# Local attention in blocks of 32 queries by 64 keys: scores on eight TensorE tiles, values on four, one PSUM bank for all fills

## The chip, the cores and the metric

One core of one Trainium2 chip. The metric is the device time of one execution in microseconds (us), the median of three runs. The core has TensorE (PE, matrix products), VectorE (DVE), ScalarE (ACT), GpSimd (POOL) and SyncE (SP, which issues DMA transfers). TensorE writes into PSUM, which has eight banks of 128 partitions by 512 fp32 numbers; the others read PSUM and on-chip memory. Each engine works off its own program in order and waits on semaphores for the others. An fp32 product shows as two records in the trace.

## What is computed

The kernel is a chain of eight stages on x of 8 sequences x 256 tokens x 128 features, each as `x = x + layernorm(stage(layernorm(x)))`: a memory-augmented attention, a linear split, a linear attention, a mixture of experts, a Mamba layer, a grouped-query attention block, a latent attention ("mla") and, last, the local transformer that the change is about. Of that last one, for each of six layers:

```python
DIM, DEPTH, HEADS, DIM_HEAD, WINDOW = 128, 6, 16, 64, 32
DIM_INNER, QK_SCALE = int(DIM * 4 * 2 / 3), 8.0        # 341
...
def look(t):                       # each window of 32 keys and the one before it
    p = jnp.pad(t, ((0, 0), (0, 0), (1, 0), (0, 0), (0, 0)))
    return jnp.concatenate([p[:, :, :nw], p[:, :, 1:]], axis=3)
bk2, bv2 = (look(bk), look(bv))
mask = (it < jb) | (it > jb + w) | (jb == -1)
sim = jnp.einsum('bhwie,bhwje->bhwij', bq, bk2) * QK_SCALE
sim = jnp.where(mask, -jnp.finfo(sim.dtype).max, sim)
attn = jax.nn.softmax(sim, -1)
out = jnp.einsum('bhwij,bhwje->bhwie', attn, bv2)
...
q = l2norm(q) * qs                 # then rotary embedding; k likewise
...
xn = (x - mu) / jnp.sqrt(var + 1e-05) * g + bln
a, gate = jnp.split(xn @ W1 + b1, 2, -1)
return a * jax.nn.gelu(gate, approximate=False) @ W2 + b2
```

## The kernel before

**Units and steps.** The local stage (`stage_local`) runs 48 units, one for each layer and sequence. A unit `n` has eight steps `p = 0..7`, one for each pair of heads; step `s = 8n + p`. Parts of several units are under way at once: in step `s` the program makes raw q or k rows for the part `s + 16` (two units ahead), turns the rows of part `s + 5`, makes the scores of `s`, turns the probabilities of `s - 2` and makes the values of `s - 3`.

**TensorE's program in a step, in this order.** The mask (L3115, one bf16 product of 384 columns that puts the bias into the score bank), eight score products (L3118: blocks of 64 queries by 96 keys for two heads, on 64x64 tiles of the array, two at a time), early fills, four flips of probabilities (L403, `table,xn`) and four of rows (L403, `table,scratch`), half the output projection at p = 2 and 3 (L3145), the centering at p = 5 (L3150), eight value products (L3162: 128 keys by 64 features, on 128x64 tiles), late fills, and last the raw rows (L3176, 512 columns). Fills are the products of the layer's other work: V (L3068, p = 4 to 7), moment (L3073), ones (L3078), gates (L3083), third (L3088, L3089), linear (L3092) and out (L398, three products). Gates, linear and third are the parts of the gated MLP of width 341 = 128 + 128 + 85, and third holds both halves of the last 85.

**Banks.** Raw rows have bank 0; the scores of step s bank 2 + s % 2; turned probabilities bank 4; turned rows bank 5; values and centering share bank 6. Fills have two banks: 7 for project, third, ones and moment, 1 for the rest. `Bench.plan` puts down for each fill which semaphore tells that its bank has been read, and `wait_free` waits for that of the fill before in the same bank.

**VectorE in a step.** Exponent sum of s - 1 with its reciprocal (L3326, L3328), rope on the raw rows (L3277, L3279, L3280), maximum of the scores (L3340), squared lengths (L3360) and small work of the MLP and residuals (L3352, L3370, L3377, L3384, L3385). At p = 5 and 7 it runs the inverse root of a row of lengths (`dve_root`, L3299 to L3311, twelve operations, each waiting for the one before), after the lengths.

**ScalarE in a step.** Square of the raw rows (L3226, the last reader of the raw bank: TensorE's next raw product waits on `squared`), copy of the turned probabilities (L3231), four exponentials (L3236), copy of the turned rows (L3248), copy of the sums (L3253), copies of V (L3191), and at p = 0 three gelus of a unit (L3209), for which the activation table is loaded, and loaded back for the next exponentials. **GpSimd** adds the rope's halves (L3432), divides the probabilities (L3425) and scales rows by the inverse root (L3439). **SyncE** moves parts of V to other partitions, three transfers in a unit.

Of the kernel before, what the change touches and what calls it, by code (L numbers as in the profile page):

```python
# [7 lines left out]
P = 128  # L8
F32 = mybir.dt.float32
U32 = mybir.dt.uint32  # L10
BF16 = mybir.dt.bfloat16
# [12 lines left out]
EPS = 1e-5  # L24
# [93 lines left out]
def layout(i):  # L118
# [42 lines left out]
    for l in range(DEPTH):  # L161
# [6 lines left out]
        out[f"layer{l}"] = [("wqkv", a[m + "Wqkv"][l]), ("wo", chunks(a[m + "Wo"][l])), ("w1", w1),  # L168
# [7 lines left out]
def tables():  # L176
# [9 lines left out]
    def near(b):  # L186
        i, j = np.arange(P)[:, None] % 64, np.arange(96)[None, :] - 32
        return np.where((j <= i) & (j >= i - LWIN) & (64 * b + j >= 0), 0, NEG).astype(f)
# [4 lines left out]
            ("band", np.concatenate([near(b) for b in range(4)], axis=1))]  # L193
# [264 lines left out]
def dve_see(M, first, n, signal, k):  # L458
# [6 lines left out]
    M.seen = first + n  # L465

# [127 lines left out]
def stage_titan(M):  # L594
# [388 lines left out]
    def pool_program():  # L983
        M.wait_loaded(pool, "titan")
        nc.gpsimd.tensor_copy(xT[:, TOKENS:], w("memT")).then_inc(S("mem_copied").up(), 1)
# [379 lines left out]
def act_rows(A, s):  # L1365
# [4 lines left out]
    for g in range(4):  # L1370
        if 0 <= u < A.units:
            n = 4 * u + g
            act.wait_ge(S("bounded"), n // 2)
# [13 lines left out]
def dve_rows(A, s):  # L1387
    M, nc, dve, S = A.M, A.M.nc, A.M.dve, A.M.sig
    for n in range(4 * s, 4 * s + 4):
        if s < A.units:  # L1390
# [5 lines left out]
            for t in range(2):  # L1396
                half = x[:, SEQ * t:SEQ * t + SEQ]
                nc.vector.tensor_tensor_reduce(half, half, A.factor[:, SEQ * t:SEQ * t + SEQ], A.scale, -3.0e38, ALU.mult, ALU.max,
                                               A.low[s % 3][:, 2 * g + t:2 * g + t + 1]).then_inc(dve.link(), 1)
            if g % 2:  # L1400
                pair = A.low[s % 3][:, 2 * g - 2:2 * g + 2]
                dve.settle()
                nc.vector.tensor_scalar(pair, pair, -1.0, None, ALU.mult).then_inc(S("bounded").up(), 1)
# [1561 lines left out]
BLOCKS, QB, KB = 4, 64, 96  # L2965
PAIRS_L = LHEADS // 2
WIDTH = BLOCKS * KB


def stage_local(M):  # L2970
# [18 lines left out]
    rows, V = M.ring(2, 8, 512), M.ring(2, BLOCKS, LIN)  # L2989
    KT, QT = M.ring(2, PAIRS_L, KB - QB + SEQ), M.ring(2, PAIRS_L, SEQ)  # L2990
    sines, sq = M.alloc(512), M.ring(2, 512)
    E, probs, turned, sums = M.ring(2, BLOCKS, KB), M.ring(2, BLOCKS, P), M.ring(2, BLOCKS, P), M.ring(PAIRS_L, SEQ)
    small, lengths = M.ring(4, 2, BLOCKS), M.ring(2, 3, 66)
    rope = M.ring(2, 4, 2, LDIM)
    xc, sq2, fed, dg, gl = M.alloc(SEQ), M.alloc(SEQ), M.alloc(SEQ), M.alloc(2, P), M.alloc(3, SEQ)
    ident, mask = M.alloc(P // 2).bitcast(BF16), M.alloc(WIDTH // 2).bitcast(BF16)
# [7 lines left out]
    score_bank = lambda s: M.bank(2 + s % 2)[:, 0:WIDTH]  # L3004
    blocks = lambda ap: ap.rearrange("p (b k) -> p b k", b=BLOCKS)
    over_keys = lambda ap: ap.unsqueeze(2).broadcast_to([P, BLOCKS, KB])
    TURNED, PARTS_T = M.bank(4), M.bank(5)

    SUMS, CENTER = M.bank(6)[:, 0:SEQ], M.bank(6)[:, SEQ:]
# [10 lines left out]


    rooms = [Bench(M, (1,)), Bench(M, (7,))]

    def bench_of(key):
        return rooms[key in ("project", "third", "ones", "moment")]

# [500 lines left out]
```

## Time and profile before

| | |
|---|---|
| median of 3 runs | 4085.57 us (4078.26 to 4090.87) |
| profiled execution | 4084.84 us, span 4083.5 us, mean granted clock of TensorE 0.937 |
| busy over the span | PE 3410.5 us (84%), DVE 2945.7 (72%), ACT 2254.4 (55%), POOL 1544.3 (38%) |
| seven stages ahead of the local one | 0 to about 1976 us |
| local stage | about 1976 to 4060 us, of it 2100 to 4000 in steady state |

A row of the timeline gives start and duration in us, the engine, the line of the kernel, the operation with the names and shapes of its output and inputs, how many records follow each other (x4), and in brackets how long the engine had been idle and what ended that. A shape such as `64*64` behind the names is the tile of the TensorE array. Busy times of TensorE overlap by the depth of its pipeline, so prices are read from start to start.

### The profile page before, as it was taken

Reading aid. Unit: us, or ns where it says so; the run is one execution under the profiler, and the core shown is the slowest. Engines: PE = TensorE matmul, PEld = TensorE weight load, DVE = VectorE, ACT = ScalarE, POOL = GpSimd, SP = SyncE. Lnnn points to the kernel's source line nnn. Section 1 sums busy time; section 2 is a strip of 40 time slices with the busy share of each in tenths; the row PEclk is TensorE's granted clock in tenths of the full one; section 3 lists DMA queues with packets and bytes.
Section 4 is the critical chain, followed back from the end, with each engine's and each line's share of the span. In section 5 each row is a group of like instructions: output and inputs, shape, how many; then the busy total and the mean of one; then the engine's idle time right before and its main releaser. Section 6 shows DMA issues by size and latency. Waiting matters only on the chain.

```text
span 4083.5 us, 78115 instructions
## 1 busy us (share of the span) xinstructions
PE 3410.5 (84%) x29021; PEld 2239.7 (55%) x29021; DVE 2945.7 (72%) x7904; ACT 2254.4 (55%) x5408; POOL 1544.3 (38%) x1445
## 2 busy tenths in 40 slices
PE   6878856457767798775799999999999999999997
PEld 4544535323234465443466666666666666666665
DVE  6465675457875455796888887887888888888875
ACT  4234433256543322686466666666666666666664
POOL 0110012436640000001655555555555555555551
PEclk9989977778889989898899999999999999999998
DMA  1000004510000000000000010001001000100000
GB/s 52 1 5 1 1 25 121 147 40 0 0 5 1 1 1 28 1 2 28 14 21 14 16 39 23 18 17 42 18 17 41 20 15 15 48 15 18 17 14 18
DMA packets 34218, 94.04 MB, mean 23 GB/s; under 512 B 5057, under 2 KB 15169, under 8 KB 32049
## 3 DMA queue, kind: packets, MB, share of 16 engines
q1 hardware_dynamic: 31312, 83.87, 7.1%
q0 software_dynamic: 2528, 5.18, 0.7%
q8 instruction: 232, 3.80, 0.4%
q14 instruction: 146, 1.19, 0.1%
HBM read 52.40 MB, written 5.18 MB: 14 GB/s over the span
## 4 chain that ended last, share of the span: by engine, by line
PE 37%; DVE 30%; ACT 15%; issue 6%; POOL 2%; DMA 1%; POOLq 0%; SPq 0%; ACTq 0%; DVEq 0%
PE psum L398 6%; PE psum L403 5%; PE psum L3145 4%; PE psum L1133 4%; PE psum L3176 3%; DVE scratch L3277 3%; ACT y L3236 3%; PE psum L1985 3%; PE psum L3162 2%; PE psum L3118 2%; DVE scratch L3326 2%; DVE scratch L3279 2%; ACT L3209 1%; ACT L3236 1%; PE psum L1187 1%
## 5 line engine op out<-in xcount | busy, mean ns | idle before, releaser
L3432 POOL TENSOR_TENSOR scratch<-scratch 128x512 f32<-128x512 f32 x384 | 489.0, 1273 | 261.0 <-DVE scratch L3280 261.0
L3425 POOL TENSOR_TENSOR xn<-y,scratch 128x384 f32<-128x384 f32 x384 | 317.6, 827 | 638.4 <-DVE scratch L3328 638.2
L3226 ACT ACTIVATE y<-psum 128x512 f32<-128x512 f32 x384 | 229.4, 597 | 592.7 <-DVE scratch L3280 592.7
L3176 PE MATMUL psum<-weights,scratch 128*128 128x512 f32 x768 | 413.7, 621 | 33.4 <-ACT y L3226 20.4
L403 PE MATMUL psum<-table,scratch 128*128 128x128 f32 (+1 forms) x2260 | 367.1, 283 | 80.3 <-ACT scratch L3248 32.0
L403 PE MATMUL psum<-table,xn 128*128 128x128 f32 x1648 | 270.7, 292 | 188.1 <-DVE xn L485 186.6
L3236 ACT ACTIVATE y<-psum,scratch 128x96 f32<-128x96 f32 x1536 | 401.8, 354 | 14.0 <-DVE scratch L3340 13.3
L3326 DVE TENSOR_REDUCE scratch<-y 128x4 f32<-128x384 f32 x384 | 211.0, 550 | 263.1 <-ACT y L3236 263.1
L3118 PEld LDWEIGHTS psum<-scratch 64*64 64x64 f32 x6144 | 265.4, 133 | 220.6 <-issue 220.6
L403 PEld LDWEIGHTS psum<-table,scratch 128*128 128x128 f32 (+1 forms) x2260 | 265.8, 145 | 140.7 <-issue 72.7
L3118 PE MATMUL psum<-scratch 64*64 64x96 f32 x6144 | 338.1, 249 | 0.0
L3277 DVE TENSOR_TENSOR scratch<-psum,weights 128x512 f32<-128x512 f32 x384 | 261.2, 680 | 81.1 <-PE psum L3176 76.3
L403 PEld LDWEIGHTS psum<-table,xn 128*128 128x128 f32 x1648 | 193.8, 147 | 228.7 <-issue 188.3
L3162 PE MATMUL psum<-xn,scratch 128*64 128x64 f32 x6144 | 263.6, 228 | 0.0
L3162 PEld LDWEIGHTS psum<-xn,scratch 128*64 128x64 f32 x6144 | 210.6, 137 | 87.8 <-issue 87.8
L3231 ACT COPY xn<-psum 128x512 f32<-128x512 f32 x384 | 223.7, 583 | 54.2 <-PE psum L403 51.6
L1133 PE MATMUL psum<-scratch 32*128 32x256 f32 (+1 forms) x2560 | 180.9, 395 | 81.6 <-DVE weights L1394 30.9
L3248 ACT COPY scratch<-psum 128x512 f32<-128x512 f32 x384 | 236.1, 615 | 1.3 <-PE psum L403 1.3
L3340 DVE TENSOR_REDUCE scratch<-psum 128x4 f32<-128x384 f32 x384 | 210.4, 548 | 8.1 <-PE psum L3118 6.7
L3176 PEld LDWEIGHTS psum<-weights,scratch 128*128 128x128 f32 x768 | 132.7, 191 | 151.8 <-issue 91.4
L3068 PE MATMUL psum<-weights,scratch 128*128 128x512 f32 x384 | 214.7, 641 | 0.0
L3439 POOL TENSOR_TENSOR scratch<-scratch,stats 128x512 f32<-128x512 f32 x192 | 200.9, 1046 | 0.0
(533 smaller groups left out, 7567.2 us busy)
## 6 DMA issues: line engine op xcount, KB each, us to landing
scratch<-scratch SPq DMA_DIRECT2D x96, 256.0 KB, 3.1
scratch<-experts_dram SPq DMA_DIRECT2D x47, 384.0 KB, 4.1
weights<-layer_dram SPq DMA_DIRECT2D x6, 1357.0 KB, 9.4
weights<-layer_dram SPq DMA_DIRECT2D x6, 1356.5 KB, 6.7
scratch<-scratch SPq DMA_DIRECT2D x48, 128.0 KB, 3.0
weights<-gqa_dram SPq DMA_DIRECT2D x2, 1738.5 KB, 8.6
results_dram<-scratch SPq DMA_DIRECT2D x11, 256.0 KB, 3.9
weights<-mamba_dram SPq DMA_DIRECT2D x2, 665.5 KB, 4.6
```

Source lines behind the costliest of these rows:

```text
L398: last = self.nc.tensor.matmul(out, a, b, start=(i == 0), stop=(i == len(pairs) - 1))
L403: return self.nc.tensor.transpose(out, src, self.c("ident")[0:k, 0:k])
L1133: last = mm(bank(n)[:, col:col + size], A.head(rows, n, at, P), A.head(cols, n, by, size), start=not A.causal, stop=True, skip_group_check ...
L3118: last = mm(bank[h:h + 64, b * KB:b * KB + KB], QT[n % 2][h:h + 64, p, b * QB:b * QB + QB], KT[n % 2][h:h + 64, p, b * QB:b * QB + KB], st ...
L3162: last = mm(SUMS[64 * h:64 * h + 64, b * QB:b * QB + QB], V[u % 2][:, b, (2 * pair + h) * LDIM:(2 * pair + h + 1) * LDIM], turned[t % 2][: ...
L3176: mm(raw_bank(a), window(m)[:, i * P:i * P + P], weight(m, "wqkv")[:, at:at + 512], start=True, stop=True).then_inc(S("rows_made").up(), 1)
L3236: last = nc.scalar.activation(E[s % 2][:, b, :], score_bank(s)[:, b * KB:b * KB + KB], ACT.Exp, bias=small[s % 4][:, 0, b:b + 1])
L3248: copy(out, PARTS_T.rearrange("p (k n) -> p k n", k=4)).then_inc(S("qk_out").up(), 1)
L3277: tt(heads(out), src, bc(cosine, LDIM), ALU.mult).then_inc(dve.link(), 1)
L3326: red(room[:, 1, :], E[t % 2], AX, ALU.add).then_inc(dve.link(), 1)
L3425: gtt(probs[t % 2][:, :, P - KB:], E[t % 2], over_keys(small[t % 4][:, 1, :]), ALU.mult).then_inc(S("divided_pool").up(), 1)
L3432: gtt(out, out, sines, ALU.add).then_inc(S("rope_sum").up(), 1)
```

## The change

In the local stage:

- A block of queries is now 32 by 64 keys (its own window and the one before). Eight blocks for two heads are 16 score products of 64 columns on tiles of 64 rows by 32 columns, of which the array has eight. They go to two banks, one for each head: 2 and 3, or 6 and 7. The mask is two bf16 products of 128 columns. Max, exponentials, sums and probabilities cover 256 numbers a row instead of 384 (four exponentials of 64 columns instead of 96).
- Probabilities fill whole rows, so that two flips turn them, not four. Values are 16 products of 32 columns on four 64x64 tiles. Their sums stand in columns 256 to 384 of banks 4 and 5, and in bank 5 those columns are also used by the turned rows; so values now also wait for the copy of the turned rows (`qk_out`), and row flips for the copy of the sums (`gathered`).
- All fills and the centering share bank 1. TensorE's step is now: mask, scores, values, early fills, raw, row flips, probability flips, late fills. Gates come early at p = 0, third late at p = 0, linear early at p = 1, ones late at p = 1, out early at p = 2, the whole projection early at p = 3, centering at p = 4, moment at p = 5. ScalarE copies the sums first and the turned probabilities last, and runs the first two gelus as an early fill. VectorE runs rope, max, exponent sum, small work, lengths, root.
- V is made as half-heads: two products on 64-column tiles (128x64 mode) into one bank, with the columns of its weights permuted on the host, and six transfers a unit by SyncE after the last V copy. The ring of sums holds nine.

Two small merges: in the first stage the statistics of x are taken before the wait for the table (and GpSimd's clears wait until x is scaled); in the mla stage the row maxima are negated once a unit (32 times) instead of twice (64).

```diff
-    rows, V = M.ring(2, 8, 512), M.ring(2, BLOCKS, LIN)
+    rows, V = M.ring(2, 8, 512), M.ring(2, 8, 512)
...
-    score_bank = lambda s: M.bank(2 + s % 2)[:, 0:WIDTH]
+    scores = lambda s: M.psum[:, 2 + 4 * (s % 2):4 + 4 * (s % 2), 0:P]
-    TURNED, PARTS_T = M.bank(4), M.bank(5)
-    SUMS, CENTER = M.bank(6)[:, 0:SEQ], M.bank(6)[:, SEQ:]
+    TURNED, PARTS_T = M.bank(4)[:, 0:SEQ], M.bank(5)
+    SUMS = M.psum[:, 4:6, SEQ:SEQ + P]
-    rooms = [Bench(M, (1,)), Bench(M, (7,))]
+    room = Bench(M, (1,))
...
         if p == 0 and unit(n - 3):
-            early.append(("third", n - 3, "gated", 2 * (n - 3)))
-            early.append(("gates", n - 3, "gelu", 2 * (n - 3)))
+            early.append(("gates", n - 3, "gelu", 3 * (n - 3) + 1))
+            late.append(("third", n - 3, "gated", 3 * (n - 3)))
         if p == 1 and unit(n - 3):
-            late.append(("linear", n - 3, "gated", 2 * (n - 3) + 1))
+            early.append(("linear", n - 3, "gated", 3 * (n - 3) + 2))
+        if p == 1 and unit(n - 2):
+            late.append(("ones", n - 2, "scaled", n - 2))
-        if p == 3 and unit(n - 3):
+        if p == 2 and unit(n - 3):
             early.append(("out", n - 3, "fed", 2 * (n - 3) + 1))
...
-            mm(bank, window(n)[:, i * P:i * P + P], weight(n, "wqkv")[:, 2 * LIN + 512 * half:2 * LIN + 512 * half + 512],
-               start=True, stop=True).then_inc(S("v_made").up(), 1)
+            for r in range(2):
+                at = 2 * LIN + 512 * (r ^ (j // 2))
+                last = mm(bank[64 * r:64 * r + 64], window(n)[:, 64 * j:64 * j + 64], weight(n, "wqkv")[:, at:at + 512],
+                          start=True, stop=True)
+            last.then_inc(S("v_made").up(), 1)
...
-                mm(bank, ident, mask, start=True, stop=False, skip_group_check=True)
-                for b in range(BLOCKS):
-                    for h in (0, 64):
-                        last = mm(bank[h:h + 64, b * KB:b * KB + KB], QT[n % 2][h:h + 64, p, b * QB:b * QB + QB],
-                                  KT[n % 2][h:h + 64, p, b * QB:b * QB + KB], start=False, stop=True, skip_group_check=True)
+                for h in range(2):
+                    mm(scores(s)[:, h, :], ident, mask, start=True, stop=False, skip_group_check=True)
+                for i in range(8):
+                    j, q = divmod(i, 4)
+                    for h in range(2):
+                        on = slice(64 * h, 64 * h + 64)
+                        last = mm(scores(s)[QB * q:QB * q + QB, h, 64 * j:64 * j + 64], QT[n % 2][on, p, i * QB:i * QB + QB],
+                                  KT[n % 2][on, p, i * QB:i * QB + 2 * QB], start=False, stop=True, skip_group_check=True)
                 last.then_inc(S("scored").up(), 1)
...
                 pe.wait_ge(S("copied"), t)
+                pe.wait_ge(S("qk_out"), min(s + 4, PARTS - 1))
...
+                for q in range(4):
+                    for j in range(2):
+                        for h in range(2):
+                            r = h ^ j
+                            last = mm(SUMS[64 * h:64 * h + 64, j, QB * q:QB * q + QB],
+                                      V[u % 2][64 * r:64 * r + 64, 4 * j + q, pair * LDIM:(pair + 1) * LDIM],
+                                      turned[t % 2][64 * r:64 * r + 64, j, QB * q:QB * q + QB], start=True, stop=True)
```

What moved shows at three places. On TensorE, from the scores of p = 7 to the mask of p = 0, in a unit in the middle of the stage, there stood (L403 is the helper that flips, `xn` the probabilities, `scratch` the rows; L3068 is V, L3176 raw):

```order
L3118 MATMUL psum<-scratch 64x96 x8
L403 MATMUL psum<-table,xn 128x128 [waits copied,divided_pool]
L403 MATMUL psum<-table,xn 128x128 x3
L403 MATMUL psum<-table,scratch 128x128 [waits qk_out,normed]
L403 MATMUL psum<-table,scratch 128x128 x3
L3162 MATMUL psum<-xn,scratch 64x64 [waits gathered]
L3162 MATMUL psum<-xn,scratch 64x64 x7
L3068 MATMUL psum<-weights,scratch 128x512 [waits v_out]
L3176 MATMUL psum<-weights,scratch 128x512 [waits squared]
L3115 MATMUL psum<-weights,scratch 128x384 [waits exped]
```

Now, from the last flips of p = 7 through V (L3087), mask (L3144), scores (L3149), values (L3164) and gates (L3113) of p = 0 to its raw product (L3177):

```order
L406 MATMUL psum<-table,y 128x128 [waits divided_pool]
L406 MATMUL psum<-table,y 128x128
L3087 MATMUL psum<-weights,scratch 64x512 [waits v_out]
L3087 MATMUL psum<-weights,scratch 64x512
L3144 MATMUL psum<-scratch 128x128 [waits exped]
L3144 MATMUL psum<-scratch 128x128
L3149 MATMUL psum<-scratch 32x64 x16
L3164 MATMUL psum<-xn,scratch 64x32 [waits qk_out,copied]
L3164 MATMUL psum<-xn,scratch 64x32 x15
L3113 MATMUL psum<-weights 128x256 [waits affine,v_out]
L3113 MATMUL psum<-weights 128x256
L3177 MATMUL psum<-weights,scratch 128x512 [waits squared]
```

The raw product with its wait on `squared` has moved from the end of a step to behind the values and early fills of the next.

On ScalarE at p = 0 there stood, from the square to the three gelus (L3209) behind both copies:

```order
L3226 ACTIVATE y<-psum 128x512 [waits lens,roped]
L3231 COPY xn<-psum 128x512 [waits turned]
L3236 ACTIVATE y<-psum,scratch 128x96 [waits divided_pool,bounded]
L3236 ACTIVATE y<-psum,scratch 128x96 x3
L3248 COPY scratch<-psum 128x4x128 [waits rows_turned]
L3253 COPY xnT<-psum 128x256 [waits projected,valued]
L3209 ACT_TABLE_LOAD [waits down]
L3209 ACTIVATE table<-psum,weights 128x256 [waits up]
L3209 ACTIVATE table<-psum,weights 128x256
L3209 ACTIVATE table<-psum,weights 85x256
```

Now, with square L3242, sums copy L3247, exponentials L3253, gelus L3225, rows copy L3265 and turned copy L3270:

```order
L3242 ACTIVATE y<-psum 128x512 [waits lens,roped]
L3247 COPY xn<-psum 128x256 [waits projected,valued]
L3253 ACTIVATE scratch<-psum,scratch 128x64 [waits divided_pool,bounded]
L3253 ACTIVATE scratch<-psum,scratch 128x64 x3
L3225 ACT_TABLE_LOAD [waits down]
L3225 ACTIVATE weights<-psum,weights 128x256 [waits up]
L3225 ACTIVATE weights<-psum,weights 128x256
L3265 COPY scratch<-psum 128x4x128 [waits rows_turned]
L3270 COPY y<-psum 128x256 [waits turned]
L3225 ACTIVATE weights<-psum,weights 85x256 [waits up]
```

The table load and two gelus have moved ahead of both copies, and the third gelu waits for a product of its own.

On VectorE around the root at p = 7, before, the operations behind the root's last (L3311) were the exponent sum and then the rope:

```order
L3311 SCALAR_TENSOR_TENSOR xnT<-xnT 128x34 [waits dve_linked]
L3326 TENSOR_REDUCE scratch<-y 128x4 [waits exped]
L3328 RECIPROCAL scratch<-scratch 128x4 [waits dve_linked]
L3277 TENSOR_TENSOR scratch<-psum,weights 128x512 [waits rows_turned,rows_made]
L3279 TENSOR_TENSOR scratch<-psum,weights 128x8x32 [waits rope_sum]
L3280 TENSOR_TENSOR scratch<-psum,weights 128x8x32
L3340 TENSOR_REDUCE scratch<-psum 128x4 [waits scored]
```

Now, from the max of the scores at p = 7 (L3339) to the root's first two (L3311, L3313 of the new lines):

```order
L3339 TENSOR_REDUCE scratch<-psum 128x4 [waits scored]
L3345 TENSOR_REDUCE scratch<-scratch 128x4 [waits exped]
L3347 RECIPROCAL scratch<-scratch 128x4 [waits dve_linked]
L3394 TENSOR_REDUCE xnT<-y 128x8 [waits squared]
L3311 TENSOR_SCALAR xnT<-xnT 128x34 [waits var_out,lens]
L3313 TENSOR_SCALAR xnT<-xnT 128x34 [waits dve_linked]
```

The exponent sum has moved from behind the root and ahead of the rope to behind the max and ahead of the root.

## Rows read from the trace of the kernel before

**Rows 1.** Windows, 2100 to 4000: us, busy of each engine, PEclk, DMA share, GB/s.

```profile
2100.00:4000.00 1900.00, 1836.99 (x17445) 1258.64 (x17442) 1528.19 (x3980) 1286.79 (x3345) 1092.00 (x1071) 1.00 0.09 23
```

**Rows 2.** Waits of TensorE from 2100 to 4000: total, times, longest.

```profile
PE psum L403 <- ACT scratch L3248: 30.9, 45, 1.1
PE psum L3092 <- ACT table L3209: 25.9, 44, 1.1
```

**Rows 3.** Timeline of TensorE over one unit.

```profile
2805.25 0.33 PE L3115 MATMUL psum<-weights,scratch 128*128 128x384 bf16 x1
...
2832.52 0.66 PE L3088 MATMUL psum<-table,weights 128*85 128x256 f32 x2
...
2833.45 1.03 PE L3083 MATMUL psum<-table,weights 128*128 128x256 f32 x4
2834.32 0.60 PE L403 MATMUL psum<-table,xn 128*128 128x128 f32 x4
...
2836.09 1.13 PE L3176 MATMUL psum<-weights,scratch 128*128 128x512 f32 x2
2837.05 0.33 PE L3115 MATMUL psum<-weights,scratch 128*128 128x384 bf16 x1
2837.30 0.88 PE L3118 MATMUL psum<-scratch 64*64 64x96 f32 x16
2838.11 0.66 PE L403 MATMUL psum<-table,xn 128*128 128x128 f32 x4
...
2839.13 0.69 PE L3162 MATMUL psum<-xn,scratch 128*64 128x64 f32 x16
2840.41 1.13 PE L3092 MATMUL psum<-table,weights 128*128 128x256 f32 x4 [0.58 <-ACT table L3209]
...
2848.49 0.33 PE L3115 MATMUL psum<-weights,scratch 128*128 128x384 bf16 x1
```

**Rows 4.** Timeline of VectorE around the root at p = 7.

```profile
2829.16 0.67 DVE L3360 TENSOR_REDUCE stats<-y 128x8 f32<-128x512 f32 x1
2829.75 0.15 DVE L3364 TENSOR_SCALAR stats<-psum 128x2 f32<-128x2 f32 x1
2830.01 0.18 DVE L3299 TENSOR_SCALAR stats<-stats 128x34 f32<-128x34 f32 x1
...
2833.39 0.55 DVE L3326 TENSOR_REDUCE scratch<-y 128x4 f32<-128x384 f32 x1
...
2834.06 0.68 DVE L3277 TENSOR_TENSOR scratch<-psum,weights 128x512 f32<-128x512 f32 x1
...
2835.32 0.55 DVE L3340 TENSOR_REDUCE scratch<-psum 128x4 f32<-128x384 f32 x1
```

**Rows 5.** Timeline of ScalarE at p = 0.

```profile
2835.43 0.60 ACT L3226 ACTIVATE y<-psum 128x512 f32<-128x512 f32 x1 [3.37 <-DVE scratch L3280]
...
2836.39 1.05 ACT L3236 ACTIVATE y<-psum,scratch 128x96 f32<-128x96 f32 x4
...
2838.22 1.28 ACT L3209 ACT_TABLE_LOAD   x1
2839.51 1.20 ACT L3209 ACTIVATE table<-psum,weights 128x256 f32<-128x256 f32 x3
```

**Rows 6.** Timeline of TensorE behind a wait for raw, and windows there.

```profile
2059.55 1.13 PE L3176 MATMUL psum<-weights,scratch 128*128 128x512 f32 x2 [2.33 <-ACT y L3226]
2060.51 0.33 PE L3115 MATMUL psum<-weights,scratch 128*128 128x384 bf16 x1
...
2064.76 1.12 PE L3176 MATMUL psum<-weights,scratch 128*128 128x512 f32 x2
...
2061.00:2064.40 3.40, 3.40 (x32) 2.85 (x30) 3.24 (x8) 1.81 (x5) 2.14 (x3) 0.50 0.02 5
```

**Rows 7.** Window over one line's tiled products of an earlier stage.

```profile
55.00:56.02 1.02, 1.01 (x32) 0.81 (x32) 1.00 0.00 0
```

**Rows 8.** Timeline of VectorE at the program's start.

```profile
12.41 3.19 DVE L438 BATCH_NORM_STATS2 stats<-x 128x6 f32<-128x128 f32 x16 [12.41 <-DMA table<-table_dram]
```

**Rows 9.** The negations of the mla stage, L1403.

```profile
L1403 DVE TENSOR_SCALAR scratch<-scratch x64: 169/169/172, 1673.8 to 1884.7; 128x4 f32<-128x4 f32 x64
```

More of the change, by code:

```diff
@@ L3019, in part @@
         return a // 8, a % 8 // 4, a % 4 // 2, a % 2
-    rooms = [Bench(M, (1,)), Bench(M, (7,))]
-    def bench_of(key):
-        return rooms[key in ("project", "third", "ones", "moment")]
+    room = Bench(M, (1,))
     def room_of(key, n):
-        return bench_of(key).bank((key, n))
+        return room.bank((key, n))
     def fills(s):
@@ L3062, in pe_fill @@
             j = int(key[1])
-            i, half = divmod(j, 2)
             if n < BATCH:
@@ L3138, in pe_program @@
-            if p in (2, 3) and 0 <= n - 1 < UNITS:
-                u = n - 1
-                out = room_of("project", u)[:, 0:SEQ]
-                if p == 2:
-                    bench_of("project").wait_free(pe, ("project", u))
-                for pair in range(4 * p - 8, 4 * p - 4):
-                    pe.wait_ge(S("gathered"), 8 * u + pair)
-                    mm(out, weight(u, "wo")[:, pair * DIM:(pair + 1) * DIM], sums[pair], start=(pair == 0),
-                       stop=(pair == 7), skip_group_check=True).then_inc(S("projected").up(), 1)
@@ L3177, in pe_program @@
                     S("rows_made").up(), 1)
+            k = s + 5
+            if 0 <= k < PARTS:
+                m, q = divmod(k, 8)
+                pe.wait_ge(S("normed"), k)
+                pe.wait_ge(S("qk_out"), k - 1)
+                pe.wait_ge(S("gathered"), min(s - 3, STEPS - 1))
+                for j in range(4):
+                    last = M.flip(PARTS_T[:, j * P:j * P + P], rows[m % 2][:, q, j * P:j * P + P])
+                last.then_inc(S("rows_turned").up(), 1)
+            t = s - 2
+            if 0 <= t < STEPS:
+                pe.wait_ge(S("divided_pool"), t)
+                pe.wait_ge(S("copied"), t - 1)
+                pe.wait_ge(S("gathered"), s - 3)
+                for j in range(2):
+                    last = M.flip(TURNED[:, j * P:j * P + P], probs[t % 2][:, 2 * j:2 * j + 2, :].rearrange("p h k -> p (h k)"))
+                last.then_inc(S("turned").up(), 1)
+            for key, f, _, _ in late:
+                pe_fill(key, f)
         pe.wait_ge(S("fed"), 2 * UNITS - 1)
@@ L3234, in act_program @@
                 act.wait_ge(S("divided_pool"), s - 2)
-                for b in range(BLOCKS):
-                    last = nc.scalar.activation(E[s % 2][:, b, :], score_bank(s)[:, b * KB:b * KB + KB], ACT.Exp,
-                                                bias=small[s % 4][:, 0, b:b + 1])
+                for h in range(2):
+                    for j in range(2):
+                        last = nc.scalar.activation(E[s % 2][:, 2 * j + (h ^ j), :], scores(s)[:, h, 64 * j:64 * j + 64], ACT.Exp,
+                                                    bias=small[s % 4][:, 0, 2 * h + j:2 * h + j + 1])
                 last.then_inc(S("exped").up(), 1)
@@ L3487, in build @@
         M.wait_loaded(M.dve, "x")
+        dve_see_x(M, M.x)
         for _, e in M.four:
```

289 lines of the change are left out of this document (132 added, 157 removed).

## Prediction

> **What bounds the kernel now.** I read the windows first: they tell which engine has no room, and at which clock. From 2100 to 4000 us, inside the local stage, TensorE is busy for 1837 of 1900 us at granted clock 1.00, VectorE for 1528 and ScalarE for 1287 [rows 1]. TensorE is the bound, and only its own work or its waits can move the stage. The list of its waits comes next: 30.9 us for the copy of the turned rows and 25.9 us for a gelu, over 44 units [rows 2]. The idle time is 63 us over 1900/43.24 = 43.9 units, 1.43 us in each. The unit of 43.24 us is the distance of two masks eight steps apart, the first and last of [rows 3]; so TensorE works for 41.8 us in it. The stage has 48 units, and 1 us in a unit is worth 48 us of 4085. That is the whole case: how much work goes, and how many waits come.
>
> **Work that goes.** One step's prices are distances between starts in [rows 3]. Mask: 2837.05 to 2837.30, 0.25; two of 128 columns instead of one of 384 give about 0.20, -0.05. Scores: 0.81 for 16 records. The raw product does 2x512 columns in 0.96, with one change of tile shape in it: 0.084 us for 100 columns. 8 rounds of two tiles with 96 columns are then 0.65, and 0.16 is start and change of shape. Of the new scores, 32 records on eight tiles are 4 rounds of 64 columns, 0.22 + 0.16 = 0.38 if the records start almost together, 1.02 + 0.16 if they go at the pace of the fastest run of tiled records, 32 in 1.02 us [rows 7]. That run has 128 columns in each record on four tiles, 8 rounds of 0.108 = 0.86, so columns and not the issue explain it; I take 0.46, near the lower end, -0.35. Values: 0.62 (busy 0.69). New are 32 records on four tiles with half the columns, 0.41 if columns set it, 0.66 if loading 64-wide weights does as now, 1.02 + at the pace of [rows 7]; I take 0.65, +0.03. Flips: eight in 1.02 (2838.11 to 2839.13) with a change of shape; six without one are 0.65, -0.37, since the shapes now change three times in a step and not four. That is -0.74 a step, -5.9 a unit. V goes to two 64-column tiles and so changes the shape twice: I take +0.24 for each of four, +1.0. Work falls to 41.8 - 4.9 = 36.9 us. The other moved fills have the same columns.
>
> The Trainium skill's page "TensorE: Matmul & The Clock Gate" speaks on both sides of this. Its Part 3 ("The mechanism") has packed tiles start about 4 ns apart, and its section "Wait — 56ns, not 53.3ns?" says that start-to-start never drops below about 25 ns. By the first the scores would stay near 0.4; by the second 32 records would be 0.8, +0.34 for scores and +0.15 for values, an estimate of +3.9 us a unit before any wait is hidden. No row here settles it.
>
> **Waits that come.** The raw rows have one bank, and a raw product waits until VectorE's rope and ScalarE's square have read the one before. Before, raw stood last in the step; now it is third. VectorE now finishes root, lengths and exponent sums before it comes to the next rope. From the end of the scores at p = 7: max about 0.34 (0.55 busy for 384 elements, now 256), exponent sum with reciprocal 0.54 (0.67 for 384: 2833.39 to 2834.06), lengths 0.59, root 3.38 (2830.01 to 2833.39), rope until the square can start 1.37, square 0.65 [rows 4, 5]: 6.9 us. In that time TensorE has values 0.65, raw 0.96, flips 0.65, V 1.1, mask 0.20, scores 0.46, values 0.65, gates 0.87 (2833.45 to 2834.32) = 5.5. **Wait 1.4 at p = 0.** Before, 8.0 us of work stood there (flips 1.02, values 0.62, V and raw 1.9, mask 0.25, scores 0.81, third and gates 1.80 from 2832.52 to 2834.32, flips 0.96, values 0.62), more than the chain, and the raw product at 2836.09 shows no wait [rows 3]. At p = 6 the root of p = 5 comes after the moments: values 0.65, the new early moment with its read 0.9, lengths 0.59, root 3.38, rope 1.37, square 0.65 = 7.4, against 5.1 of work. **Wait 2.3.**
>
> One bank for the fills. At p = 0 third needs the bank in which the gates stand until two gelus have read them. ScalarE gets to them from the square that released raw by way of sums copy 0.26, four exponentials 0.85 (1.05 busy for 96 columns), table load 1.29, two gelus 0.75 [rows 5]: 3.2 us against raw and flips, 1.6. **Wait 1.6.** Linear at p = 1 needs third's product to be read by VectorE, after max and exponent sum: 1.35 after the scores against values 0.65, **0.7**. Out at p = 2 needs the ones read in the same place, **0.7**. Values at p = 3 and 4 wait for copies that ScalarE's late gelus push back, **0.4**. Sum 7.1 (today linear waits 0.58 for a gelu [rows 3]). The unit is 36.9 + 7.1 = 44.0 us, +0.76, times 48: **+36 us**. The ends: 3.7 us of waits (raw alone) to 9.
>
> **The clock.** Where raw waited 2.33 us at 2059.55, the granted clock of the next 3.40 us was 0.50, the 1.2 GHz level [rows 6]. From mask to the next raw went 4.25 us (2060.51 to 2064.76), against 2.70 undisturbed (2837.05 to 2839.13, and 0.62): 1.55 us lost. Waits of up to 1.1 us [rows 2] left the clock at 1.00 [rows 1]. The new wait at p = 6 has the size of the first; with 1.4 and 1.6 behind it I take one such loss in each unit: **+74 us**. The ends are 0 and two in a unit, 149.
>
> **The small merges.** 16 statistics of x ran for 3.19 us after the table had come [rows 8]; before it, if x is there first, they cost nothing: -3, between -5 and 0. 64 negations of 169 ns [rows 9] become 32 in a stretch that VectorE sets; at 0.17 us for each that goes: -5, between -10 and +2, since the bias is ready one group later.
>
> **Sum.** On the profiled execution's 4084.8 us (0.7 below the median): + 36 + 74 - 8 = **4187 us**.
>
> **Rivals.** (A) The forecast: waits and clock, 4130 to 4240, chance 0.40. (B) The waits without the clock: 4113; for it speaks that 2.3 is just where the trace has one such case; 0.15. (C) Records don't start together: at 32 ns each scores and values cost 0.9 more in a step, 7.1 in a unit, work 44.0. The work between shadows the chains, so waits fall to 3.8 (p = 0 0.2, p = 6 1.1, third 1.6, linear and out 0.35 each, values 0.2) and the clock holds: 47.8, +219 - 8, 4296; down to 4240 where only one of the two is so slow; 0.15. The skill's floor of 25 ns is this rival's rule. (D) **Faster.** The place is the fill bank and the order on ScalarE: if gelus, third's product and ones are read in time, and only raw waits with 3.7 and values 0.4, the unit is 41.0: -107 - 8, 3970. If the root hides as well, and today's 1.43 is all, it is 38.3: -237 - 8, 3840. It decides at 6.3 us of waits in a unit, 0.8 under my sum, with the clock held; against it stand the sums of each chain above. 0.20, most of it near 3970 to 4060. (E) Waits of 6.3 to 6.6 with the clock held, or a gain that a few slow stretches eat: within 12 us of before; 0.10.
>
> **How the numbers follow.** 0.3% is 12 us, about what a measurement of this kernel can tell from no change. Slower is A, B and C, 0.70; same E, 0.10; faster D, 0.20. The range from 4050 to 4290 holds A, B, E and most of C; it leaves out most of D and what lies above C's middle, about 2 in 10.
>
> **What would show it.** In the changed profile: mask-to-mask distances of 45 to 46 us; TensorE busy for clearly less than 97% of 2100:4000 and its clock at 0.93 to 0.97; in the list of waits raw first (on ScalarE's square, about 3.7 us a unit), then third on a gelu, linear and out on VectorE; scores in 0.46 from start to start. Scores and values of 1.0 each mean C. A list of waits under 6 us a unit with clock 1.00 means D. The forecast is wrong above all if VectorE reaches the rope earlier than I count, because one of the six terms of the chain is shorter, or if the clock doesn't drop after 2.3 us.

## The result and the profile after

The changed kernel takes 4155.93 us (median of 4 runs, 4145.65 to 4159.23) against 4082.11 for the kernel before (4 runs, 4078.26 to 4090.87): a ratio of 1.0173 with a 95% interval of 1.0148 to 1.0199, +74 us. It is slower by 1.7%, clear of the noise, and 31 us less so than the 4187 forecast. The profiled execution took 4156.27 us, its span is 4154.8.

The windows of the same stretch as [rows 1], 2100 to 4000 us (us, busy of PE, PEld, DVE, ACT and POOL, PEclk, DMA share, GB/s):

```profile
2100.00:4000.00 1900.00, 1573.96 (x27582) 1029.43 (x27578) 1397.93 (x3854) 1169.19 (x3215) 973.29 (x1035) 0.99 0.12 28
```

TensorE was busy for 1837 us of these and is now for 1574, with 58% more records. Work did go. What came is in the list of TensorE's waits in the same stretch (total, times, longest), to be set beside [rows 2]:

```profile
PE psum L3177 <- ACT y L3242: 163.4, 127, 2.3
PE psum L3117 <- ACT weights L3225: 61.0, 42, 1.5
PE psum L401 <- DVE weights L3370: 40.4, 42, 1.0
PE psum L3121 <- DVE weights L3358: 38.9, 42, 1.0
PE psum L3164 <- ACT xn L3270: 10.1, 43, 0.2
PE psum L3164 <- ACT y L3270: 9.9, 42, 0.2
```

Raw (L3177) leads, then third, out, linear and values: 323.7 us in 42.3 units (of 44.93 us on average), 7.7 in each, where 1.43 us were idle before. The timeline of TensorE shows each in its place; it answers to [rows 3]:

```profile
2835.20 0.28 PE L3144 MATMUL psum<-scratch 128*128 128x128 bf16 x2
2835.41 0.45 PE L3149 MATMUL psum<-scratch 64*32 64x64 f32 x32
2835.79 0.67 PE L3164 MATMUL psum<-y,scratch 64*64 64x32 f32 x32
2836.45 1.13 PE L3177 MATMUL psum<-weights,scratch 128*128 128x512 f32 x2
2837.41 0.60 PE L406 MATMUL psum<-table,scratch 128*128 128x128 f32 x4
2837.85 0.38 PE L406 MATMUL psum<-table,y 128*128 128x128 f32 x2
2838.16 1.08 PE L3087 MATMUL psum<-weights,scratch 128*64 128x512 f32 x4
2839.17 0.29 PE L3144 MATMUL psum<-scratch 128*128 128x128 bf16 x2
...
2842.92 1.12 PE L3177 MATMUL psum<-weights,scratch 128*128 128x512 f32 x2 [1.42 <-ACT y L3242]
...
2846.17 0.67 PE L3117 MATMUL psum<-weights 128*85 128x256 f32 x2 [1.46 <-ACT weights L3225]
...
2847.10 0.28 PE L3144 MATMUL psum<-scratch 128*128 128x128 bf16 x2
...
2849.28 1.13 PE L3121 MATMUL psum<-weights 128*128 128x256 f32 x4 [0.92 <-DVE weights L3358]
...
2854.42 1.57 PE L401 MATMUL psum<-weights 128*128 128x256 f32 x6 [0.96 <-DVE weights L3370]
...
2876.89 1.12 PE L3177 MATMUL psum<-weights,scratch 128*128 128x512 f32 x2 [2.29 <-ACT y L3242]
...
2891.53 0.27 PE L3144 MATMUL psum<-scratch 128*128 128x128 bf16 x2
```

From mask to mask a unit now takes 44.43 us (2847.10 to 2891.53) against 43.24, and 46.0 in the 14 of 43 units in which the clock drops. The first rows are a step at p = 7 without a wait: from start to start scores take 0.38, values 0.66 (0.60 in the steps where a fill follows them and not raw), flips 0.75 (0.65 where the mask follows them and not V), V 1.01.

Where the 71.3 us between the two spans came from, by landmarks of the two timelines (the last product of the mla stage, the first and the last mask, the end):

| stretch | before | after | difference |
|---|---|---|---|
| to the last product of the mla stage | 1901.28 | 1887.64 | -13.6 |
| to the first mask of the local stage | 74.87 | 70.29 | -4.6 |
| first mask to last mask | 2046.13 | 2118.87 | +72.7 |
| last mask to the end | 61.2 | 78.0 | +16.8 |

Of the +72.7, +71.4 lie in the 43 steady units; the first three units are 3.1 us shorter than before and the last two 4.4 longer.

### The profile page after: what moved, and what is told of

It is laid out like the page before. It is cut to its first block, busy times and chain, and to the rows that moved or that the text cites. A ratio compares the mean times of both kernels' runs of the same rounds, so it can differ in the third digit from the quotient of the medians.

```text
span 4154.8 us, 102703 instructions
## 1 busy us (share of the span) xinstructions
PE 3208.4 (77%) x41309; PEld 2044.0 (49%) x41309; DVE 2843.3 (68%) x7872; ACT 2177.6 (52%) x5408; POOL 1447.6 (35%) x1443
## 3 DMA queue, kind: packets, MB, share of 16 engines
q14 instruction: 146, 1.19, 0.1%
## 4 chain that ended last, share of the span: by engine, by line
PE 40%; DVE 30%; ACT 12%; issue 6%; POOL 3%; DMA 1%; POOLq 0%; SPq 0%; ACTq 0%; DVEq 0%
PE psum L401 6%; PE psum L3093 4%; PE psum L3177 4%; PE psum L406 4%; PE psum L1145 3%; DVE scratch L3289 3%; DVE xnT L3394 3%; PE psum L1998 3%; PE psum L3087 2%; PE psum L1199 2%; PE psum L3164 2%; PE psum L3149 2%; DVE scratch L3292 2%; DVE scratch L3291 2%; PE psum L3121 1%
## 5 line engine op out<-in xcount | busy, mean ns | idle before, releaser
L3177 PE MATMUL psum<-weights,scratch 128*128 128x512 f32 x768 | 434.9, 650 | 196.7 <-ACT y L3242 189.8
L406 PEld LDWEIGHTS psum<-table,scratch 128*128 128x128 f32 (+1 forms) x2284 | 286.3, 146 | 301.3 <-issue 223.1
L3265 ACT COPY scratch<-psum 128x512 f32<-128x512 f32 x384 | 224.9, 586 | 374.8 <-PE psum L406 374.3
L406 PE MATMUL psum<-table,scratch 128*128 128x128 f32 (+1 forms) x2284 | 373.0, 285 | 47.5 <-DVE scratch L2699 11.8
L3242 ACT ACTIVATE y<-psum 128x512 f32<-128x512 f32 x384 | 229.3, 597 | 329.3 <-DVE scratch L3292 328.9
L3447 POOL TENSOR_TENSOR scratch<-scratch,xnT 128x512 f32<-128x512 f32 x384 | 400.9, 1044 | 0.0
L3289 DVE TENSOR_TENSOR scratch<-psum,xnT 128x512 f32<-128x512 f32 x384 | 263.6, 686 | 66.1 <-PE psum L3177 53.9
L3339 DVE TENSOR_REDUCE scratch<-psum 128x4 f32<-128x256 f32 x384 | 160.6, 418 | 198.9 <-PE psum L3149 198.9
L3177 PEld LDWEIGHTS psum<-weights,scratch 128*128 128x128 f32 x768 | 129.5, 195 | 265.2 <-ACT y L3242 232.2
L3394 DVE TENSOR_REDUCE xnT<-y 128x8 f32<-128x512 f32 x384 | 257.3, 670 | 2.7
L3087 PE MATMUL psum<-weights,scratch 128*64 128x512 f32 x768 | 214.2, 637 | 0.4 <-ACT stats L3217 0.4
L3253 ACT ACTIVATE scratch<-psum,scratch 128x64 f32<-128x64 f32 x768 | 180.9, 333 | 1.3 <-DVE scratch L3339 1.3
L3253 ACT ACTIVATE y<-psum,scratch 128x64 f32<-128x64 f32 x768 | 179.4, 324 | 0.8 <-DVE scratch L3339 0.2
L3149 PE MATMUL psum<-scratch 64*32 64x64 f32 x12288 | 177.6, 225 | 0.0
L406 PE MATMUL psum<-table,y 128*128 128x128 f32 x784 | 155.7, 284 | 22.0 <-DVE y L495 20.8
L406 PE MATMUL psum<-table,xn 128*128 128x128 f32 x112 | 25.3, 420 | 183.4 <-DVE xn L495 183.4
L3291 DVE TENSOR_TENSOR scratch<-psum,xnT 128x256 f32<-128x256 f32 x384 | 159.0, 414 | 2.4 <-POOL scratch L3434 2.4
L3292 DVE TENSOR_TENSOR scratch<-psum,xnT 128x256 f32<-128x256 f32 x384 | 158.9, 414 | 0.0
```

The costliest lines, as they stand in the source:

```text
L406: return self.nc.tensor.transpose(out, src, self.c("ident")[0:k, 0:k])
L3087: last = mm(bank[64 * r:64 * r + 64], window(n)[:, 64 * j:64 * j + 64], weight(n, "wqkv")[:, at:at + 512], start=True, stop=True)
L3149: last = mm(scores(s)[QB * q:QB * q + QB, h, 64 * j:64 * j + 64], QT[n % 2][on, p, i * QB:i * QB + QB], KT[n % 2][on, p, i * QB:i * QB + 2 ...
L3177: mm(raw_bank(a), window(m)[:, i * P:i * P + P], weight(m, "wqkv")[:, at:at + 512], start=True, stop=True).then_inc(S("rows_made").up(), 1)
L3253: last = nc.scalar.activation(E[s % 2][:, 2 * j + (h ^ j), :], scores(s)[:, h, 64 * j:64 * j + 64], ACT.Exp, bias=small[s % 4][:, 0, 2 * h ...
L3289: tt(heads(out), src, bc(cosine, LDIM), ALU.mult).then_inc(dve.link(), 1)
```

## The experiments

The theory was that three things make the kernel slower against 4.9 us a unit of saved work: the inverse root on VectorE, now in the chain that raw waits for; the one bank for all fills; and the clock behind the longest wait. The rivals were that these waits are only names for one loop through VectorE and ScalarE, and that raw's place alone is at fault.

**A shorter root.** Two of three Newton iterations are left out, so the inverse lengths are less exact:

```diff
-        for i in range(3):
+        for i in range(1):
```

> The changed kernel, with one Newton iteration in the inverse root of the local stage instead of three (six operations of 0.23 us fewer at p = 5 and p = 7, 1.38 us each; the precision of the inverse lengths suffers, nothing else changes). Theory (VectorE's root is in the chain that raw waits for): the wait at p = 6 falls from 2.28 to about 0.9, that at p = 0 from 1.42 to about 0.05, the waits for third (1.46), linear (0.92) and out (0.96) stay, the clock no longer drops; a unit of 44.43 becomes 41.7 and the whole 4156 - 48*2.75 - 22 = about 4000. Rival (the waits come from ScalarE's order, the root is hidden beside it): unit and time stay within 10 us of 4156.

Measured: 3990.63 us in one execution, and 41.69 us a unit, where 41.7 was expected. TensorE's waits, 2100 to 3900:

```profile
PE psum L3117 <- ACT weights L3225: 64.8, 44, 2.0
PE psum L3177 <- ACT y L3242: 46.2, 85, 1.3
PE psum L401 <- DVE weights L3370: 41.5, 43, 1.3
PE psum L3121 <- DVE weights L3358: 40.3, 44, 1.0
```

Raw's wait fell from 3.9 to 1.1 us a unit, the others stayed, and the clock held up to 3857 us. 2.76 us less root in the chain is 2.74 us less unit: the root stands in it with its full length.

**Third and out in other columns.** The scores fill 128 of the 512 columns of their banks:

```diff
+    rooms = {"third": Bench(M, (2,)), "out": Bench(M, (6,)), "": Bench(M, (1,))}
...
+    def half(key, j):
+        return M.bank({"third": 2, "out": 6}[key] + j)[:, SEQ:]
...
+                if p == 2 and n >= 3:
+                    pe.wait_ge(S("gated"), 3 * (n - 3))
+                if p == 3 and n >= 3:
+                    pe.wait_ge(S("fed"), 2 * (n - 3) + 1)
```

> The changed kernel, with third and out taken out of the one fill bank: third goes to columns 256 to 512 of banks 2 and 3, out to those of bank 6, which the scores leave free; each waits for the exponentials that last read its bank, and the masks of p = 2 and p = 3 wait for their readers. Theory (one bank for all fills makes the waits for third, linear and out): all three go, 1.46 + 0.92 + 0.96 = 3.34 us a unit, raw keeps its 3.7: unit 41.1, time about 4156 - 160 = 3996, between 3980 and 4030. Rival (the waits are for ScalarE and VectorE as such, the bank only names them): third's gelu and product come as late as before and the masks, linear or out wait instead; less than 1 us a unit is won, 4110 or more.

Both products also wait now for the exponentials that last read their bank. Measured: 4030.69 us, at the upper end of what was expected; ratio to the kernel before 0.9863 (0.9844 to 0.9882). Waits of TensorE, 2100 to 3900:

```profile
PE psum L3187 <- ACT y L3252: 163.9, 126, 2.3
PE psum L3174 <- ACT y L3280: 45.3, 84, 0.9
PE psum L3174 <- ACT xn L3280: 12.5, 47, 0.5
```

The waits for third, linear and out are gone, 3.3 us a unit, and raw's are as before. Of the gain 0.9 comes back: values at p = 1 (L3174) now wait 0.85 us for a copy behind ScalarE's gelus. A unit is 41.70 us, 2.7 less: 2.4 of these are the listed waits, and for the other 0.3 no row here gives a reason. But the clock drops in 22 of the 43 steady units instead of 14, and these take 43.1 to 44.5 us. From the last mask to the end it is 57.5 us instead of 78.0: there, with no attention to put between, the one bank strings the fills one behind the other. Part of the difference is the clock: TensorE is busy for 31.7 us of it at a mean clock of 0.71, and in the changed kernel for 45.3 us at 0.57, with as many records (269).

**The root in parts.** With third and out moved, the two roots are cut into parts, in the order they had:

```diff
-        m, half = (n + 1, 1) if p == 5 else (n + 2, 0)
+        m, half = (n + 1, 1) if p < 5 else (n + 2, 0)
...
+        rounds = {2: (-1, 0), 4: (1, 2), 5: (-1,), 6: (0,), 7: (1, 2)}.get(p)
```

Here -1 stands for the first three operations and 0 to 2 for the iterations.

> The kernel with third and out in the free columns, and its two inverse roots cut into parts: the root of p = 5 runs its first six operations at p = 2, long after its lengths are there, and the rest at p = 4; that of p = 7 runs three operations at p = 5, three at p = 6 and six at p = 7. The same operations in the same order. Theory (raw waits only where more than about 1 us of root stands in one step): waits for raw fall from 3.7 to about 0.5 us a unit, the clock holds, the wait of 0.85 for values at p = 1 stays; unit 41.7 - 3.2 = 38.5, time 4031 - 154 - 30 = 3847, between 3820 and 3900. Rival (spread over the steps the root shifts VectorE in every step, and exponentials and values wait for it): 3950 or more.

Measured: 3903.23 us, ratio 0.9567 (0.9546 to 0.9587), 4.3% below the kernel before. A unit is 39.79 us (40.73 in one of eight) at clock 1.00. Waits, 2100 to 3800:

```profile
PE psum L3187 <- ACT y L3252: 73.5, 175, 0.6
PE psum L3174 <- ACT y L3280: 46.8, 85, 1.3
PE psum L3174 <- ACT xn L3280: 12.8, 48, 0.5
```

56 us above the point of what was expected, and 3 above its range, mostly because 1.7 us a unit of raw's waits stay, not 0.5: they are now four of 0.2 to 0.6 at p = 4 to 7, and values wait 1.4, as in the run before. With 3.1 us of waits in a unit of 39.79 the work is 36.7 us.

**The root in parts alone,** with all fills still in one bank:

> The changed kernel, with the two inverse roots cut into parts as in the run with free columns (at p = 2 and 4, and at p = 5, 6 and 7), and all fills still in one bank. Theory (raw waits and fill waits add up, each has its own cause): raw waits fall from 3.8 to about 1.7 us a unit as they did there, the fill waits of 3.3 stay, no stretches at half clock: unit 42.4, time 4156 - 48*2.05 - 23 = 4035, between 4015 and 4050. Rival (one feeds the other: with the root spread, VectorE comes later to the products of third and linear and the fill waits grow): 4060 or more.

Measured: 4043.23 us, ratio 0.9895 (0.988 to 0.9911), inside the expected range, 42.54 us a unit, and no steady unit at half clock. Raw waits 69.0 us over 2100 to 3800 (1.7 a unit); third, out and linear 58.1, 38.4 and 37.1, as in the changed kernel. So root and bank add up, 1.9 and 2.7 us a unit.

**Idle products against the clock.**

```diff
+            if p in (6,) and 0 <= s < STEPS:
+                pe.wait_ge(S("exped"), s - 1)
+                for j in range(3):
+                    mm(M.bank(6)[:, SEQ:], c("ident"), weight(n, "wqkv")[:, 0:SEQ], start=True, stop=True)
```

> The changed kernel, with three idle products of 256 columns (0.43 us each, their result is read by nobody) on TensorE at p = 6, ahead of the wait for raw, so that the 2.28 us wait is cut to about 1.0 us without anything else coming earlier. Theory (a wait of 2.3 us costs a stretch at half clock in one unit of three, 1.58 us each time, about 16 of 48 units): no stretch at granted clock 0.5 between 2100 and 4000, a unit always 44.43, time 4156 - 22 = 4134, between 4125 and 4142. Rival (the 46.0 us units have another cause, or the products delay raw): time stays at 4150 to 4160 or rises.

Measured: 4130.79 us, 25 below the changed kernel; by the ratios to before (1.0128, 1.0107 to 1.0149, and 1.0173) it is 18 us. Up to the last unit a steady unit takes 44.4 to 44.6 us. One of them, not none as expected, still has a stretch at half clock, which costs it 0.2 us. In the window the clock is 1.00:

```profile
2100.00:4000.00 1900.00, 1634.86 (x28115) 1078.85 (x28114) 1409.05 (x3888) 1183.83 (x3247) 982.50 (x1045) 1.00 0.12 29
```

TensorE does 1.3 us more in each unit, to no use, and the kernel gets faster. Between the two profiled executions the 43 steady units together are 21.1 us shorter, which is the price of the clock in them. Another 7.4 us are won behind the last mask, where no idle product runs (70.6 us at clock 0.69, against 78.0 at 0.57).

**Raw at the end of the step again.** All of the raw block moved behind the late fills.

> The changed kernel, with the raw product moved from behind the early fills to the end of the step, where it stood before; all else is as changed. Theory (its place is what exposes the root): between the scores of p = 7 and the raw product of p = 0 there are now flips, V, raw of p = 7, mask, scores, values, gates, flips and third, about 6.8 us against a chain of 6.9, and at p = 6 about 6.4 against 7.4; waits for raw fall from 3.7 to about 1.1 us a unit, the fill waits stay at 3.3 or grow by what raw hid before third (third then waits 0.9 more): unit 42.7, time about 4156 - 80 - 22 = 4055, between 4020 and 4100. Rival (raw last makes VectorE begin its rope later, and max and exponentials with it): the waits only move to probabilities and fills, and the time stays within 15 us of 4156.

Measured: 4489.73 us, ratio 1.0991, far outside what theory and rival gave. One step, from mask to mask 5.34 us:

```profile
2823.89 0.27 PE L3144 MATMUL psum<-scratch 128*128 128x128 bf16 x2
...
2824.09 0.69 DVE L3289 TENSOR_TENSOR scratch<-psum,xnT 128x512 f32<-128x512 f32 x1 [2.55 <-PE psum L3196]
...
2825.48 0.60 ACT L3242 ACTIVATE y<-psum 128x512 f32<-128x512 f32 x1 [1.85 <-DVE scratch L3292]
...
2825.97 0.37 ACT L3247 COPY xn<-psum 128x256 f32<-128x256 f32 x1
...
2826.48 0.63 PE L406 MATMUL psum<-table,scratch 128*128 128x128 f32 x4 [1.33 <-ACT xn L3247]
...
2828.27 1.12 PE L3196 MATMUL psum<-weights,scratch 128*128 128x512 f32 x2
...
2829.23 0.27 PE L3144 MATMUL psum<-scratch 128*128 128x128 bf16 x2
```

Raw, rope, square, then the copy of the sums, and the row flips wait for that copy, since the sums now share a bank with the turned rows; raw stands behind the flips. I had counted the chain to raw and not the one from raw.

**Raw last and third and out moved,** both edits:

> Raw last and third and out in the free columns, both edits in one. Theory (work of 36.9 us a unit is what is left when the waits go): raw waits 1.1 to 1.6 and fills 0.2, unit 38.4 to 39.2, time about 4156 - 48*5.5 - 22 = 3870, between 3850 and 3930, below the kernel before by 5%. Rival (a chain through VectorE and ScalarE sets the unit at about 41): 3980 or more.

Measured: 4202.72 us, ratio 1.028 (1.0255 to 1.0305), where 3850 to 3930 was expected. The waits of third, linear and out are gone and the flips wait instead (L406 for L3257: 213.3 and 66.6 us over 2100 to 4000). The same loop, and the rival's side.

**Raw last, sums copied first.** ScalarE's copy of the sums ahead of the square:

> The kernel with raw last, and ScalarE's copy of the sums ahead of the square instead of behind it. The run with raw last alone was 8% slower than the changed kernel, with 2.5 us waits of the row flips for that copy (it stands behind a square that waits for the rope that waits for the raw product just made). Theory (that loop of raw, rope, square, copy and flips was all that made raw last so slow): the loop is gone, the waits for flips with it, time near what was expected of raw last, 4020 to 4100. Rival (raw last is slow as such, since max and exponentials stand behind the rope on VectorE): 4300 or more.

Measured: 4313.99 us in one execution. The waits of the flips for that copy fell from 218.5 to 40.8 us over 2100 to 3800, and third now waits up to 4.2 us, 145.1 in all against 65.5. One row of VectorE's list of waits (2100 to 3800) and one of TensorE's:

```profile
DVE scratch L3289 <- PE psum L3196: 302.8, 140, 4.8
PE psum L3117 <- ACT weights L3225: 145.1, 35, 4.2
```

The time is the rival's. VectorE's rope is first in its step and waits for the raw product just made, 2.2 us each of 140 times, with the max and so the exponentials behind it. That they are the rest of the loop I read from the order and this row; a VectorE order with max first was not tried.

**Raw early in the kernel before,** only that block moved:

> The kernel before, with only the raw product moved, from the end of the step to behind the early fills. Theory (the place of raw exposes the root in either kernel): at p = 6 TensorE has 4.6 us of work between the scores of p = 5 and raw against a chain of 7.0, wait 2.4; at p = 0 6.3 against 7.2, wait 0.9; 3.3 us a unit, +158, and stretches at half clock on top: 4244 to 4300. Rival (raw early only costs where the attention is narrow): within 20 us of 4085.

Measured: 4542.51 us in one execution, 240 to 300 above what the theory gave. Waits of TensorE, VectorE and ScalarE, 2100 to 3800:

```profile
PE psum L3130 <- ACT y L3226: 272.3, 196, 3.2
DVE scratch L3326 <- ACT y L3236: 494.6, 191, 6.0
ACT xn L3231 <- PE psum L403: 487.9, 255, 3.0
```

Raw does wait, as expected, but 196 times in some 254 steps, not only behind a root. In that kernel ScalarE copies the turned probabilities ahead of the exponentials, so it waits for flips that now stand behind raw, and VectorE's exponent sum ahead of the rope waits for those exponentials. The changed kernel has all three orders turned round together, and neither place of raw can be judged without them.

**The small merges alone,** in the kernel before:

> The kernel before, with only the two small merges: statistics of x ahead of the wait for the table (GpSimd's clears wait until x is scaled), and one negation of the row maxima a unit in the mla stage. Theory: 3.5 us at the start (the first flip of TensorE stood at 22.96 us before and at 19.51 after) and 5.2 in the mla stage (232.5 us from its first product to its last before, 227.3 after): 4081 - 9 = 4072, between 4068 and 4077. Rival (both are hidden by a DMA or another stage later on): 4081.

Measured: 4071.64 us, ratio 0.9972 (0.9961 to 0.9982), 12.2 below, with an interval of 7 to 16. TensorE's first flips start at 19.68 (before: 22.96), and the last product of the mla stage at 1888.51 (before: 1901.28), so 12.8 us are won by then, and 14.1 stand between the spans of the two profiled executions.

## Why the prediction came out

**Work per unit.** Expected 36.9 us, measured 44.43 - 7.67 = 36.8, and 36.7 in the run with the roots in parts. The parts differ a little and cancel. Scores are 0.38 and not 0.46: records on different tiles start 6 to 7 ns apart, and the last of the 32 starts 0.24 us after the first. So rival C falls. The Trainium skill's page "TensorE: Matmul & The Clock Gate" says in its section "Wait — 56ns, not 53.3ns?" that start-to-start never drops below about 25 ns; for records on different tiles the measurement is far below that, and about 4 ns from Part 3 of the page ("The mechanism") is near. The prediction said that no row could settle this, but the trace of before does. Of the tiled records from which it took a pace, four start between 55.00 and 55.03; only from one round of the tiles to the next is it 0.11 us:

```profile
55.01 0.32 PE L667 MATMUL psum<-scratch 128*32 128x128 f32 x4
```

Rival C's 32 ns was the average over such rounds. Values are 0.60 to 0.66, as forecast: half the columns, and no gain. A round of them takes 58 ns in either kernel. That loading the 64-wide weights sets this pace, as the prediction took it, fits but is not shown. Flips are 0.65, V is 1.01 against 1.1.

**Waits.** By place, expected and measured: raw at p = 0 1.4 and 1.42; raw at p = 6 2.3 and 2.28; third 1.6 and 1.46; linear 0.7 and 0.92; out 0.7 and 0.96; values 0.4 and 0.48, and 0.15 for raw at p = 4 that was not on the list. The recorded terms of the chain at p = 6 add up to 7.5 us and not to the 7.4 given for them, which makes its wait 2.4; the trace has 7.3 against 5.0 of work. Linear and out were mis-sized by 0.2 to 0.3: I let chain and work start together, but VectorE's max starts 0.20 us after the first value product at p = 1 (2847.89 and 2847.69), and at p = 2, where the rope is still ahead of it, 0.30 after. The sum is 7.7 against 7.1, and a unit +1.19 us against +0.76: 43 units make +51, not +36. That the chains are the cause, and not names for something else, is what the short root (-2.74 us a unit), the free columns (-2.7) and both kinds together (-4.64) show.

**The clock.** The term that was mis-sized most. The price of one stretch at half clock was right, 1.55 expected and 46.01 - 44.43 = 1.58 measured. The count was not: I took one in each unit, it was 14 of 43, so +22 us against +74, and the clock of the window was 0.99, not 0.93 to 0.97. The windows show two units next to each other, each with a wait of 2.28 or 2.29 us ahead of its second window:

```profile
2830.90:2834.30 3.40, 3.40 (x10) 1.93 (x12) 2.05 (x5) 1.47 (x6) 2.22 (x3) 0.51 0.00 0
2877.30:2880.70 3.40, 3.40 (x78) 1.81 (x76) 1.99 (x5) 2.46 (x8) 3.04 (x4) 1.00 0.00 0
```

The same wait with the same work around it cost a stretch once and not the other time. The fourteen units are seven pairs of neighbours, five or seven units from pair to pair, and the wait at p = 6 is 2.28 or 2.29 us in all 43: its length alone doesn't tell whether the clock falls. In the run with third and out moved raw waits as long, and it is 22 of 43.

I called 2059.55 the one such case in the trace of before. It had three waits of raw of this size, all ahead of the steady units. At 2017.15 (2.43 us) the clock fell to 0.50 as well, but behind the longest of them, with other work around it, it did not:

```profile
1980.36 1.12 PE L3176 MATMUL psum<-weights,scratch 128*128 128x512 f32 x2 [2.50 <-ACT y L3226]
...
1981.90:1985.30 3.40, 2.47 (x23) 1.29 (x21) 2.87 (x7) 1.98 (x6) 2.88 (x4) 1.00 0.01 2
```

So "one in each unit" stood on one row where two others were at hand. The idle products measured what the clock costs in the steady units, 21 us.

**What was not in the sum.** The tail: +16.8 us from the last mask to the end, at a mean clock of 0.57 against 0.76 before. The six kernels with all fills in one bank take 70.6 to 78.7 us for it, the three with third and out moved 56.4 to 57.5, less than before the change. I had priced the one bank in the steady units only. The head of the local stage, -4.6 us, has fewer areas to clear and earlier raw products; no run isolates it. The merges alone brought 12.2 us; the 8 lies within the interval of 7 to 16. In that run's trace the part in the mla stage is 5.2 as expected, 3.3 are at TensorE's first flips, and another 4.3 are won by its last product of the first stage (256.51 against 264.07), and these 7.6 us stand when the mla stage begins. Why these 4.3, no run tells.

So 51 + 22 - 14 - 5 + 17 = 71 us stand against 36 + 74 - 8 = 102 forecast. The sign and the mechanism of the waits were right. That the number came as near as it did is in part luck: the forecast had 52 us too much for the clock and 11 too little gain at the start, and against that 15 too little for the waits and 17 for the tail. The kernel stands between (A), one loss in each unit, and (B), none.

**Rival D.** It did not come true for the changed kernel. The edits made its conditions, and the kernel became faster than before as soon as either was met: 0.9863 with the fills moved, 0.9895 with the root in parts, 0.9567 with both. The gains are smaller than D gave (4031 against 3970, 3903 against 3840), since values wait 1.4 us a unit and not 0.4, the clock drops in half of the units in the first, and part of raw's wait stays in the second. The point from which it decides, 6.3 us of waits in a unit, fits: the short root, the moved fills and the root in parts alone have 5.0, 5.3 and 5.6 us of waits a unit and are faster.

## What to carry to other kernels

Saved work on the busiest engine is worth what the chains of the others leave of it: before making that engine's part shorter, add up for each of its semaphore waits the chain on the other engines and the work that now stands in its shadow, since a shorter step lengthens every wait by as much. Long serial pieces of another engine (here a root of twelve dependent operations) should be cut so that no step holds more than the shadow is long, and a buffer that several users share should be looked at for the last of its readers. The orders of the engines are one thing: moving one product alone cost 8 to 11% here in either kernel.

## What the runs showed of the hardware

Score records on eight 64x32 tiles start 6 to 7 ns apart within a round of tiles at full clock, and all 32 within 0.24 us. Value products with half the moving columns (32 instead of 64) on twice as many tiles took 0.60 us against 0.62, no less.

The kernel ran faster with 1.3 us of useless products in each unit: 4130.79 against 4155.93 us.

Some operations of VectorE take many times as long while GpSimd works. Its first integer operation in the program took 2.64 us beside GpSimd's three clears in the kernel before. With the merges VectorE comes to it 3.5 us earlier, ahead of them, and it takes 0.17 (L414). But the clears begin when they did, since they wait for the first of eight scalings of x and not for all, and now the third and fourth scaling take 3.05 and 2.82 us beside them, the others 0.33 to 0.35. The first two rows are of the kernel before, the others of the changed one:

```profile
16.60 2.73 POOL L987 MEMSET scratch<- 128x1024 f32 x3
16.72 2.64 DVE L411 TENSOR_SCALAR stats<-stats 128x16 uint32<-128x16 uint32 x1
...
13.22 0.17 DVE L414 TENSOR_SCALAR stats<-stats 128x16 uint32<-128x16 uint32 x1
...
15.73 4.66 DVE L495 TENSOR_SCALAR xn<-x,stats 128x128 f32<-128x128 f32 x8
16.49 2.73 POOL L999 MEMSET scratch<- 128x1024 f32 x3
```

The root of the local stage has the same in it. Its second operation (L3313, changed kernel) ran 99 times: 47 times with GpSimd idle, in 0.17 to 0.19 us, and 52 times beside GpSimd, in 0.97 at the median. In 46 of those 47 the first operation (L3311) is the long one instead, 0.98 us at 2871.49. So about 0.8 us of each root of 3.4 is time beside GpSimd, in the chain that raw waits for. No run moves it.
